# The convolution's SiLU products on GpSimd and its history as a bias

## The reference

```
x = x + 0.5 * ffn(layernorm(x))
x = x + mamba(layernorm(x))          # mamba has its own layernorm and its own residual
x = x + 0.5 * ffn(layernorm(x))

mamba(x):
  xs, z = split(layernorm(x) @ W_in.T)                 # 2 x 1024 channels
  xc    = silu(b_conv + sum_k xs[t - 3 + k] * W_conv[:, k])   # 4 taps, causal
  dt, B, C = split(xc @ W_xproj.T)                     # 32, 16, 16
  delta = softplus(dt @ W_dt.T + b_dt)
  h     = exp(delta * A) * h + delta * B * xc          # scan over t, 16 states per channel
  y     = sum_n C * h + D_skip * xc
  out   = (y * silu(z)) @ W_out.T + x
```

## Time and profile before

| | |
|---|---|
| median of 3 runs | 5120.74 us (5119.88 to 5122.5) |
| profiled execution | 5123.48 us |
| its span | 5120.9 us |
| VectorE busy | 4631.6 us, 90% |
| TensorE matmul busy | 4387.8 us, 86% |
| ScalarE busy | 3013.0 us, 59% |
| GpSimd busy | 2897.6 us, 57% |

### The profile page before, as it was taken

How to read it: one execution, slowest core, us unless ns; L and a number is a source line. 1 busy time by engine, 2 the same in 40 slices (tenths; PEclk the granted TensorE clock), 3 DMA queues, 4 the chain that set the end, 5 groups by cost and what they waited for, 6 DMA issues and landing times.

```text
span 5120.9 us, 59521 instructions
## 1 busy us (share of the span) xinstructions
PE 4387.8 (86%) x16640; PEld 2481.4 (48%) x16640; DVE 4631.6 (90%) x5826; ACT 3013.0 (59%) x6291; POOL 2897.6 (57%) x2111
## 2 busy tenths in 40 slices
PE   6777889898889888889888889889889898889777
PEld 2344545454554545545454554545545454554443
DVE  2799999999999999999999999999999999999992
ACT  2556656656666566656656665566656656665552
POOL 1555656465565656556465565556556465565661
PEclk9888999998999989999998999989999998999788
DMA  1545555454655546556465555546555465654551
GB/s 62 151 138 175 163 168 175 137 183 151 180 165 157 170 147 184 160 169 176 137 185 150 180 165 160 167 147 185 164 167 172 136 185 150 180 165 138 171 155 63
DMA packets 423066, 810.80 MB, mean 158 GB/s; under 512 B 41264, under 2 KB 41264, under 8 KB 418640
## 3 DMA queue, kind: packets, MB, share of 16 engines
q1 hardware_dynamic: 422736, 807.00, 53.1%
HBM read 772.25 MB, written 34.60 MB: 158 GB/s over the span
## 4 chain that ended last, share of the span: by engine, by line
PE 38%; DVE 35%; issue 11%; ACT 10%; POOL 2%; DMA 2%; DVEq 0%; SPq 0%; POOLq 0%; ACTq 0%
DVE decay L1067 16%; DVE g L1077 10%; PE mm L422 8%; PE y_acc L506 7%; PE mm L448 7%; PE mm L433 6%; DVE xc L1021 3%; PE mm L529 2%; PE mm L411 2%; PE mm L470 2%; PE mm L458 2%; ACT decay L851 2%; ACT rows L664 2%; DMA res_scratch<-rows 1%; POOL dbx L1285 1%
## 5 line engine op out<-in xcount | busy, mean ns | idle before, releaser
L1285 POOL TENSOR_TENSOR dbx<-u,b_all 128x1024 f32<-128x1024 f32 x1024 | 2411.8, 2358 | 1833.6 <-DVE decay L1067 1830.6
L1067 DVE TENSOR_TENSOR_SCAN decay<-decay,state,dbx 128x512 f32<-128x512 f32 x2048 | 2620.9, 1280 | 235.0 <-ACT decay L851 207.4
L506 PE MATMUL y_acc<-ident,g 128*128 128x128 f32 x8192 | 1207.5, 289 | 354.6 <-DVE g L1077 344.6
L851 ACT ACTIVATE decay<-delta,neg_a 128x512 f32<-128x512 f32 x2048 | 1415.6, 692 | 68.4 <-ACT state L857 0.4
L506 PEld LDWEIGHTS y_acc<-ident,g 128*128 128x128 f32 x8192 | 1007.0, 149 | 882.0 <-DVE g L1077 504.9
L1077 DVE TENSOR_TENSOR g<-decay,c_all 128x512 f32<-128x512 f32 x2048 | 1374.3, 671 | 2.0 <-PE y_acc L506 2.0
L857 ACT ACTIVATE state<-decay 128x1 f32<-128x1 f32 x2048 | 338.7, 166 | 1246.1 <-DVE g L1077 1244.0
L433 PE MATMUL mm<-wbuf_c,col 128*128 128x512 f32 x1024 | 459.9, 592 | 0.9 <-DVE rows L1010 0.9
L448 PE MATMUL mm<-xn_col,wbuf_a 128*128 128x512 f32 x512 | 299.7, 741 | 69.0 <-ACT delta L810 48.5
L448 PE MATMUL mm<-xn_col,wbuf_d 128*128 128x512 f32 x512 | 290.7, 721 | 37.0 <-ACT col L729 35.3
L1021 DVE SCALAR_TENSOR_TENSOR xc<-mm,conv_sb,xc 128x509 f32<-128x509 f32 (+2 forms) x384 | 285.4, 743 | 30.0 <-ACT xs_last L776 20.9
(11 more groups left out here) (92 smaller groups left out, 4271.0 us busy)
## 6 DMA issues: line engine op xcount, KB each, us to landing
b_all<-bc_scratch SPq DMA_DIRECT2D x1024, 256.0 KB, 3.7
c_all<-bc_scratch SPq DMA_DIRECT2D x1024, 256.0 KB, 4.4
wbuf_c<-in_w_v SPq DMA_DIRECT2D x32, 1024.0 KB, 8.2
wbuf_d<-in_w_r SPq DMA_DIRECT2D x16, 1024.0 KB, 6.6
xin<-in_x SPq DMA_DIRECT2D x16, 1024.0 KB, 10.3
wbuf_c<-in_w_k SPq DMA_DIRECT2D x16, 1024.0 KB, 8.0
wbuf_d<-in_w_in SPq DMA_DIRECT2D x16, 1024.0 KB, 7.5
wbuf_a<-in_w_in SPq DMA_DIRECT2D x16, 1024.0 KB, 10.4
```

Source lines behind the costliest of these rows:

```text
L506: last = pe.matmul(y_acc[:, tb, j * P:(j + 1) * P], g[:, m % GRING, tb * P:(tb + 1) * P], ident[:, :], start=n == 0 and j == 0 and tb % 2 ...
L851: act.activation(decay[:, m % DBANKS, :], delta[:, q % 2, j, :], ACT.Exp, scale=neg_a[:, QT * q + j, n:n + 1]).then_inc(decay_done, 1)
L1067: dve.tensor_tensor_scan(d, d, dbx[:, s % DBX, j, :], state[:, batch, m:m + 1], ALU.mult, ALU.add).then_inc(scan_done, 1)
L1285: pool.tensor_tensor(dbx[:, s % DBX, :, :], u[:, q % 2, :, :], b_all[:, s % BRING, :].unsqueeze(1).broadcast_to([P, QT, W]), ALU.mult).the ...
```

## The change

Seven of the eight SiLU products (tiles 0 to 6) are moved from VectorE to GpSimd, as plain products of two tiles. The one is added to the tanh by ScalarE first, in a pass of its own that waits for the tanh. GpSimd does product e in its step 36 + 2e; tile 7 stays as it was, on VectorE in step 48. The head is no longer added by VectorE: GpSimd adds the convolution's bias to it once per chunk (`h5`), and ScalarE's first pass is cut in four, 509 columns with the bias as before and three single columns whose bias is the head. The waits are moved to a new set of marks, `s_pool`.

```diff
 def conv_start(k, e, batch):      # ScalarE
-    act.wait_ge(m_pool.sem, m_pool.at(k, "h4"))
+    act.wait_ge(m_pool.sem, m_pool.at(k, "h5"))
...
-    act.activation(xc2[:, e, :], bank(f"xs{e}"), ACT.Identity, scale=conv_sb[:, e, KC - 1:KC],
+    src = bank(f"xs{e}")
+    act.activation(xc2[:, e, HIST:W], src[:, HIST:W], ACT.Identity, scale=conv_sb[:, e, KC - 1:KC],
                    bias=evec[:, 0, e:e + 1]).then_inc(m_act.sem, 1)
+    for c in range(HIST):
+        act.activation(xc2[:, e, c:c + 1], src[:, c:c + 1], ACT.Identity,
+                       scale=conv_sb[:, e, KC - 1:KC],
+                       bias=head[:, e, c:c + 1]).then_inc(m_act.sem, 1)
...
 def conv_tanh(k, e):              # ScalarE
-    act.wait_ge(m_dve.sem, m_dve.at(k, f"head{e}"))
+    act.wait_ge(m_dve.sem, m_dve.at(k, f"c2_{e}"))
     if e >= TB:
-        act.wait_ge(m_dve.sem, m_dve.at(k, f"silu{e - TB}"))
-    act.activation(rows[0][:, e % TB, :], xc2[:, e, :], ACT.Tanh, scale=0.5).then_inc(m_act.sem, 1)
+        act.wait_ge(s_pool.sem, s_pool.at(k, f"{e - TB}"))
+    t = rows[0][:, e % TB, :]
+    act.activation(t, xc2[:, e, :], ACT.Tanh, scale=0.5).then_inc(m_act.sem, 1)
+    if e < 7:
+        act.wait_ge(m_act.sem, m_act.at(k, f"th{e}"))
+        act.activation(t, t, ACT.Identity, bias=1.0).then_inc(m_act.sem, 1)
...
 def conv_taps(k, e):              # VectorE
...
-    dve.wait_ge(m_pool.sem, m_pool.at(k, "h4"))
-    dve.wait_ge(m_dve.sem, m_dve.at(k, f"c2_{e}"))
-    dve.tensor_tensor(xc2[:, e, 0:HIST], xc2[:, e, 0:HIST], head[:, e, :],
-                      ALU.add).then_inc(m_dve.sem, 1)
...
-                    if front and s in (34, 36, 38, 40, 42, 44, 46, 48):
-                        conv_silu(f, (s - 34) // 2)
+                    if front and s == 48:
+                        conv_silu(f, 7)
...
 def conv_head(k, batch):          # GpSimd
...
+    pool.wait_ge(m_pool.sem, m_pool.at(k, "h4"))
+    pool.tensor_tensor(head[:, :, :], head[:, :, :],
+                       evec[:, 0, :].unsqueeze(2).broadcast_to([P, ET, HIST]),
+                       ALU.add).then_inc(m_pool.sem, 1)
...
+def conv_silu(k, e):              # GpSimd
+    pool.wait_ge(m_act.sem, m_act.at(k, f"one{e}"))
+    o = xc2[:, e, :]
+    pool.tensor_tensor(o, rows[0][:, e % TB, :], o, ALU.mult).then_inc(s_pool.sem, 1)
...
+                    if front and s in (36, 38, 40, 42, 44, 46, 48):
+                        conv_silu(f, s // 2 - 18)
```

More of the change, by code:

```diff
@@ L146, in build @@
         m_act = Marks(sem("mamba_act"), "in0 in1 in2 in3 res0 res1 res2 res3 xn0 xn1 xn2 xn3 "
-                      "tap0 last0 tap1 last1 th0 tap2 last2 th1 tap3 last3 th2 tap4 last4 th3 "
-                      "tap5 last5 th4 tap6 last6 th5 tap7 last7 th6 th7 xp")
+                      + " ".join(f"tap{e} col0_{e} col1_{e} col2_{e} last{e}" + (f" th{e - 1} one{e - 1}" if e else "")
+                                 for e in range(ET)) + " th7 xp")
         m_dve = Marks(sem("mamba_dve"), ["st0", "st1", "st2", "st3", "mv0", "mv1", "mv2", "mv3"]
-                      + ["c0_0", "c1_0", "c2_0", "head0"]
-                      + [q for e in range(1, ET) for q in (f"silu{e - 1}", f"c0_{e}", f"c1_{e}", f"c2_{e}", f"head{e}")]
-                      + ["silu7"])
+                      + [f"{q}{e}" for e in range(ET) for q in ("c0_", "c1_", "c2_")] + ["silu7"])
         m_pool = Marks(sem("mamba_pool"), ["v", "v2"] + newton + ["mean", "shift", "one",
-                       "h0", "h1", "h2", "h3", "h4"])
+                       "h0", "h1", "h2", "h3", "h4", "h5"])
+        s_pool = Marks(sem("silu_pool"), "0 1 2 3 4 5 6")
         h_pe = Marks(sem("quarter_pe"), "dt0_0 dt0_1 sk0 dt1_0 dt1_1 sk1 dt2_0 dt2_1 sk2 dt3_0 dt3_1 sk3")
@@ L462, in xproj @@
             def xproj(it, k, part):
-                pe.wait_ge(m_dve.sem, m_dve.at(k, f"silu{4 * part + 3}"))
+                pe.wait_ge(s_pool.sem, s_pool.at(k, f"{3 + 3 * part}"))
+                if part == 1:
+                    pe.wait_ge(m_dve.sem, m_dve.at(k, "silu7"))
                 if part == 0:
@@ L658, in ffn_norm @@
                         act.wait_ge(m_dve.sem, count)
+                        act.wait_ge(s_pool.sem, s_pool.at(k - 1, "6"))
                 elif fronted:
@@ L819, in skip_columns @@
                 act.wait_ge(m_dve.sem, m_dve.at(k, "silu7"))
+                act.wait_ge(s_pool.sem, s_pool.at(k, "6"))
                 for j in range(QT):
@@ L1245, in conv_head @@
             def conv_head(k, batch):
-                if due(count := m_dve.at(k - 1, "head7")):
-                    pool.wait_ge(m_dve.sem, count)
+                if due(count := m_act.at(k - 1, "last7")):
+                    pool.wait_ge(m_act.sem, count)
                 if due(count := m_act.at(k - BATCHES, "last7")):
@@ L1267, in make_u @@
                 pool.wait_ge(m_dve.sem, m_dve.at(k, "silu7"))
+                pool.wait_ge(s_pool.sem, s_pool.at(k, "6"))
                 pool.tensor_tensor(u[:, q % 2, :, :], delta[:, q % 2, :, :], xc2[:, QT * q:QT * q + QT, :],
                                    ALU.mult).then_inc(h_pool.sem, 1)
+            def conv_silu(k, e):
+                pool.wait_ge(m_act.sem, m_act.at(k, f"one{e}"))
+                o = xc2[:, e, :]
+                pool.tensor_tensor(o, rows[0][:, e % TB, :], o, ALU.mult).then_inc(s_pool.sem, 1)
             def ffn_add(i, k, tb):
```

## The result

The changed kernel takes 5162.15 us in the median (5158.78 to 5166.04, 4 runs) against 5120.31 for the kernel before (5116.83 to 5122.5, 4 runs). The ratio is 1.0083, with a 95% interval of 1.0065 to 1.01: slower by 42 us, where the prediction said 24 us faster. The profiled execution has a span of 5156.7 us against 5120.9.

The account below looks back on a forecast made before the run. ScalarE and TensorE bound steps 32 to 37, VectorE 38 to 41, VectorE and nearly TensorE 42 to 47. Middle chunks -20, first scanned chunk -4, lead-in -2: -26 from 5123.5, median-scaled and stated as 5096 us, range 5055 to 5135.

Parts of the forecast that it names:

- 1 and 2, what leaves VectorE: Steps 32 to 46: seven products of 0.68 us and eight head adds of 0.26 per chunk leave VectorE.
- 3, ScalarE's extra: Steps 33, 35 and 37: ScalarE's added passes cost 0.82 us per tile, so scan 38 starts 2.46 us later.
- 4, GpSimd's extra at nothing: Seven moved products, 8.9 us a chunk, and the extra head add, 0.2 us, cost nothing on GpSimd.
- rival E: A GpSimd product comes so late that the projection or a dbx product waits: 5125 us; chance 0.03.
- The rule weighed: Steps 39 and 41: longer GpSimd products slow four mix instructions by 0.08 us each per chunk, making the sum 5100.
- Rival B, TensorE's clock: Steps 32 to 37: longer TensorE waits slow z2 and xs3 through the clock, 3.0 us a chunk, 5138 us; chance 0.19.
- Steps 42 to 47: Middle chunks: TensorE closes its own waits, mean 2.0 us, so these steps go from 33.0 to about 31 us.
- the first scanned chunk: Last FFN missing, ScalarE has room: only scan 38 late, 0.8 against some five savings of 0.95, giving -4 us.
- the lead-in: Before any scan, TensorE closes waits of 0.22 to 0.82 us ahead of five xs tiles: -2 us.
- Rival A: VectorE decides everywhere, so 6.9 us of each of 16 chunks come off: 5010 us; chance 0.07.
- C: Waits ahead of xs5 and xs6 shrink; xs6 (-12) and xs3 (-24) reach full speed: 5060 us; chance 0.14.
- D: No change: ScalarE's extra at its upper bound of 1.32 us, three times, eats all savings: 5118 us; chance 0.11.

Follow-up runs that it names:

- silu_only: Kernel before with only the seven SiLU products moved to GpSimd and the added one on ScalarE, history still on VectorE: 5122.49 us, ratio 1.0003.
- history_only: Kernel before with only the history moved to ScalarE's column passes, every SiLU product still on VectorE: 5144.89 us, ratio 1.0045.
- late_product: Changed kernel with each GpSimd SiLU product issued one step later (37 + 2e instead of 36 + 2e): 5132.9 us, ratio 1.0022.
- after_filled: Changed kernel plus zero-matrix filler matmuls (9, 16, 8) in TensorE's waits ahead of xs1, xs3 and xs6: 5098.7 us, ratio 0.9956.
- no_add_of_one: Changed kernel without ScalarE's add of one, so its output differs from the reference: 5115.1 us, ratio 0.9989.
- The filled pair: Kernel before and changed kernel, each with the same zero-matrix fillers (9, 16, 8) in TensorE's waits: 5100.35 us and 5098.7 us.

## Why the prediction was wrong

**1 and 2, what leaves VectorE: right.** The sizes held. Busy time fell by 82.6 us instead of 105; 18 us of the difference are 23 mixes at 1.54 instead of 0.74 us, nearly all of which belong to point 4.

**3, ScalarE's extra: the step that failed.** Its place was right: three times on the chain in steps 32 to 37. Its size was not. Tanh and add of one cost 0.66 more together, as forecast (the +0.66 ahead of z2 in silu_only), but the three column passes take 0.71 us, not 0.15, so the passes add up to some 1.37 per tile and not 0.82. On the chain the table shows: from xs1 to z2 +1.25 (tile 1), from xs2 to xs3 +1.36 (tile 2), and step 37 +1.69, of which 0.33 is the longer xs3 and 1.36 tile 3. That is 3.97 in all, 1.32 a tile, instead of 2.46: just my upper bound. The missing 1.5 is worth 21 us in 14 chunks. history_only, where the passes stand alone, shows them ahead of z2, ahead of xs3 and in step 37 with 0.6 to 0.8 us each. I had priced a column pass by `xs_last` (0.05 to the next instruction), a copy without pointers. The nearer row was in rows 2: a full pass with two pointers takes 0.80 where one without takes 0.63. If that 0.17 is a cost per instruction and not per element, a column costs 0.05 + 0.17 = 0.22; measured 0.24. That it is the pointers was not tried by itself.

**4, GpSimd's extra at nothing: wrong by two side effects.** No product was late and no scan waited for one, as forecast (rival E did not occur). But a mix that starts while a GpSimd product runs ends only behind it. VectorE's savings in steps 38 to 41 were 2.2 us, 0.3 more than forecast, and steps 39 and 41 gave 0.73 + 0.53 of it back: 0.95 instead of 1.9, 13 us in the run. late_product, which changes only the place of the products, took 29 us off, more than these 13. Step 43, 1.2 us longer, is not part of it: no mix is slow there, VectorE waits 1.1 us for ScalarE's decay, and in after_filled, with the same products but xs6 at full speed, it takes 4.89 us again. That is TensorE's clock.

The second is GpSimd's extra head add, put into idle time that is not there: its queue runs without a gap from the head adds into the next dbx products. These come some 0.3 us later, and so does the b load that waits for them; behind it on SyncE the store of the residual is issued 0.2 us later and lands 0.5 later, and ScalarE waits for it in step 30. The rows above give that wait: 5.0 and 5.5 us in the run in the two kernels without the extra add, 12.2 and 12.1 in the two with it, even where tile 0 has no column pass. That is the +0.5 of steps 30 and 31, 7 us.

**The rule weighed.** I had priced the contention of GpSimd and VectorE at 4 x 0.08 us a chunk, from the 819 ns of the earlier trace rows. The mixes show it at +0.73 (up to 1.476 us) in step 39 of each of the 14 middle chunks and at up to +1.08 (1.824 us) in step 41 of seven. A row of before could have told: the SiLU's mean of 761 ns hides two values, 0.68 where it starts beside no GpSimd instruction and 0.81 where it starts 0.26 us before the end of a dbx. These end 0.55 us after that dbx, and so does each slowed mix of the changed kernel end 0.55 us after GpSimd's product. 0.08 was not the strength of the contention but what happened to be left of the dbx. The Trainium skill, "GPSIMD Engine Reference", section 1, lets every VectorE instruction with two SBUF inputs contend. The trace agrees: mix, SiLU and head add read both tiles from SBUF and are slowed, with the sizes above. Every instruction that reads one of its tiles from PSUM keeps its time beside GpSimd: the scans and the g products, whose decay lies in PSUM, never took more than 1.29 and 0.69 us, and the three taps from PSUM never more than 0.75.

**Rival B, TensorE's clock: it came on top.** I gave it 0.19 and 5138. Both signs that I had named for it are there: z2 at 1.2 GHz in 11 chunks (+1.33 in the mean) and a longer xs3 (+0.33), 1.7 us a chunk or 23 us. Against it I had held that the added wait was only 0.8 us; it was 1.25 ahead of z2, since step 3 was too small. The wait alone does not decide: with 2.4 us of it z2 is at full speed in all chunks of no_add_of_one and at half clock in five of history_only, with 2.5 at half clock in ten of silu_only. What differs is xs1 ahead of it. In the changed kernel z2 is fast in the three chunks whose xs1 took 6.35 to 6.69 us and slow in the others (up to 6.23); in late_product, with the same 3.08 us of wait, it is fast in five chunks with an xs1 of 6.32 to 6.52 us and slow in nine with one of up to 6.24. In history_only all five slow ones follow an xs1 of 5.4 us or less, but so do two fast ones; a rule does not come out of these rows.

**The account.** Steps 32 to 37: 3.97 + 1.33 + 0.33 = 5.6, as measured. Whole: forecast 5096, + 21 (column passes on the chain) + 7 (the store in step 30) + 13 (contention) + 23 (clock) = 5160, against 5162.15. Column passes, contention and clock were each changed by a run of their own; the split of the 5.6 is read from TensorE's rows, and the terms are not independent, as the runs of the halves show. The filled pair cuts the same loss another way: 42 us between the two kernels without fillers, none with them. By that cut half clock costs more than 23 us, since it also keeps steps 42 to 47 from giving all that VectorE saves there. A slow xs3 also lays tile 3's extra open: step 37 takes 4.89 us in both filled kernels, VectorE's own pace, and 7.39 in the changed one.

**Steps 42 to 47: right.** 33.05 to 31.11, as forecast, and so the first scanned chunk (-5.6, forecast -4) and the lead-in (-2.8, forecast -2). Rival A is out (the chain was not VectorE's), C too (xs3 and xs6 did not become faster: 5.99 to 6.32 and 5.66 to 5.87 us in the mean). D's sum, with ScalarE's extra at its upper bound, is what the chain showed for that term (3.97 against 3.96); from its 5118 the other three terms, 7 + 13 + 23, lead to 5161. So the forecast failed by three terms: one that it sized too low, the column passes, and two that it had weighed and left out or put at nothing, TensorE's clock and GpSimd's side effects.

**Still open.** Why before, silu_only and no_add_of_one, with different work, come to nearly the same 306.9 to 307.5 us in the mean middle chunk (xs1, xs3 and xs6 take up to 6.7 us instead of 3.6 in all three, so they may take up what is saved elsewhere; no run shows it); and what besides the wait and the length of xs1 decides whether z2 runs at half clock.

## What to carry to other kernels

Price a small instruction by its fixed part: find the row with the same operands (pointers, source), not the one with the same size. Move work off the bounding engine only in the stretches where it bounds; here the two edits cost 42 us on all tiles and gain 55 us on those where ScalarE has room, with the products a step later and clear of the mixes. Put GpSimd's work beside VectorE instructions that read one of their tiles from PSUM, and not beside those that read two from SBUF. When a change lengthens a wait of TensorE, count the next matmul groups at half clock too, and hold two kernels against each other with fillers in these waits to see what the work itself is worth; look whether the fillers themselves run at full speed in both.

## What was not expected of the hardware

- A VectorE instruction that reads two SBUF tiles (mix, SiLU) and starts during a GpSimd tensor_tensor ends 0.54 to 0.55 us after that ends, whatever was left of it: 0.81 us with 0.26 left, 1.47 with 0.92, 1.78 with 1.23. Eight mixes of the changed kernel that were under way for 0.02 us or more when the product started kept 0.74; three that had started 0.01 us or less before it waited (1.82). Instructions that read one tile from PSUM (scans, g products, taps) were not slowed. The 128x3 head add ended 0.02 after a dbx: 0.44 us with 0.42 left, 1.94 with 1.93 left.
- A ScalarE pass over one column with pointers for scale and bias is 0.35 us and holds the engine for 0.24; the copy of three columns without them holds it for 0.05.
- 33 filler matmuls a chunk (66 rows in the trace) in TensorE's waits make the unchanged kernel 0.4% faster, by a clock of 0.937 instead of 0.920, with no other edit.
